# Linear-attention numerators of a perceiver block: one full 128x128 stationary tile per 128 tokens in place of two half tiles

## The reference

```python
qp = exp(q @ W_feat - |q|^2 / 2) / sqrt(128)      # 16 heads of 64, 128 features
kp = exp(k @ W_feat - |k|^2 / 2) / sqrt(128)
def step(carry, qkv):                              # over the 32 tokens of a sequence
    S, z = carry
    q_t, k_t, v_t = qkv
    S = S + einsum('bhd,bhe->bhde', k_t, v_t)
    z = z + k_t
    num = einsum('bhd,bhde->bhe', q_t, S)
    den = einsum('bhd,bhd->bh', q_t, z) + 1e-6
    return ((S, z), num / den[..., None])
y = y @ Wo
```

## Time and profile before

| | |
|---|---|
| median of 3 runs | 260.74 us |
| the three runs | 260.09, 260.74, 263.33 us |
| profiled execution: device time | 261.14 us |
| profiled execution: span | 259.3 us |
| PE busy | 244.4 us, 94% |
| PE weight loads busy | 191.7 us, 74% |
| DVE busy | 186.6 us, 72% |
| ACT busy | 146.4 us, 56% |
| POOL busy | 101.5 us, 39% |

### The profile page before, as it was taken

One profiled execution on the slowest core, in us unless ns is written; L12 is line 12 of the kernel. 1 busy time (PEld: TensorE's weight loads), 2 busy tenths in 40 slices (PEclk: granted clock), 3 DMA queues, 4 the chain that ended last, 5 costly groups with the idle time before them and its releaser, 6 DMA issues.

```text
span 259.3 us, 7034 instructions
## 1 busy us (share of the span) xinstructions
PE 244.4 (94%) x2746; PEld 191.7 (74%) x2752; DVE 186.6 (72%) x474; ACT 146.4 (56%) x284; POOL 101.5 (39%) x139
## 2 busy tenths in 40 slices
PE   7979999999999999999999999999969889999984
PEld 7844467786687678777777778787758778888853
DVE  3586688676833686777887897856556879998995
ACT  1333454454445887665776667666707157877772
POOL 2161113342302568335662688365500023434430
PEclk9979799999999999999999999999979999999999
DMA  6999999970079001100110000000000000010001
GB/s 210 374 382 402 396 399 370 379 278 3 1 223 335 10 0 47 40 3 4 40 43 3 4 3 0 3 3 4 3 0 3 3 1 3 0 43 20 21 25 61
DMA packets 15378, 26.83 MB, mean 103 GB/s; under 512 B 1233, under 2 KB 8689, under 8 KB 15345
## 3 DMA queue, kind: packets, MB, share of 16 engines
q1 hardware_dynamic: 14848, 26.28, 28.3%
q10 hardware_dynamic: 496, 0.10, 0.2%
HBM read 25.33 MB, written 1.05 MB: 102 GB/s over the span
## 4 chain that ended last, share of the span: by engine, by line
PE 66%; DVE 17%; issue 5%; POOL 5%; ACT 3%; DMA 2%; SPq 0%; DVEq 0%; POOLq 0%; ACTq 0%
PE b L1331 11%; PE b L1092 7%; PE b L1373 7%; PE b L1093 6%; PE b L1094 6%; PE b L1350 5%; PE b L1254 3%; PE b L1206 3%; PE b L1250 3%; PE b L1257 3%; PE b L1172 2%; DVE yT_lo L964 2%; PE b L1503 2%; DMA xwq<-in_xWq 2%; DVE smk L910 2%
## 5 line engine op out<-in xcount | busy, mean ns | idle before, releaser
L593 ACT ACTIVATE phi<-b 128x512 f32<-128x512 f32 x48 | 26.0, 598 | 15.3 <-PE b L1331 15.3
L842 DVE TENSOR_TENSOR x_lo<-b,x_hi 128x512 fp32r<-128x512 f32 x32 | 21.7, 688 | 16.8 <-ACT x_hi L460 16.7
L343 POOL TENSOR_TENSOR lnr<-lnv,mh 128x1 f32<-128x1 f32 x16 | 8.8, 552 | 60.8 <-DVE lnv L709 60.8
L400 POOL TENSOR_TENSOR sq_lo<-sq_sum,sq_hi 128x512 fp32r<-128x512 f32 x16 | 20.6, 1287 | 25.9 <-ACT sq_hi L460 25.9
L518 ACT ACTIVATE sq<-b 128x512 f32<-128x512 f32 x32 | 19.3, 603 | 18.2 <-PE b L1094 18.2
L394 POOL TENSOR_TENSOR sq_sum<-sq,sq 128x512 f32<-128x512 f32 x16 | 20.7, 1293 | 21.7 <-ACT sq L518 21.7
L1092 PE MATMUL b<-nT_lo,wp_hi 128*128 128x512 f32 x64 | 26.8, 419 | 0.1
L1373 PEld LDWEIGHTS b<-va,smk 128*64 128x64 f32 x512 | 18.3, 142 | 11.3 <-issue 7.2
L1373 PE MATMUL b<-va,smk 128*64 128x65 f32 x512 | 21.8, 232 | 5.0 <-DVE y L932 2.8
L1093 PE MATMUL b<-nT_hi,wp_lo 128*128 128x512 f32 x64 | 25.1, 391 | 0.0
L1094 PE MATMUL b<-nT_hi,wp_hi 128*128 128x512 f32 x64 | 25.0, 391 | 0.0
(11 more groups left out here) (178 smaller groups left out, 628.6 us busy)
## 6 DMA issues: line engine op xcount, KB each, us to landing
cT<-in_ctxT SPq DMA_DIRECT2D x8, 1028.0 KB, 12.0
cn<-in_ctx SPq DMA_DIRECT2D x8, 1024.0 KB, 10.6
wv_raw<-in_aWv SPq DMA_DIRECT2D x1, 1024.0 KB, 14.2
wp_raw<-in_aWq SPq DMA_DIRECT2D x4, 256.0 KB, 4.8
wp_raw<-in_aWk SPq DMA_DIRECT2D x4, 256.0 KB, 5.0
w_raw<-in_w2T SPq DMA_DIRECT2D x1, 1024.0 KB, 5.7
wo<-in_aWo SPq DMA_DIRECT2D x1, 1024.0 KB, 8.3
w_raw<-in_w1T SPq DMA_DIRECT2D x1, 1024.0 KB, 5.1
```

What stands on the lines that cost most here:

```text
L400: nc.gpsimd.tensor_tensor(sq_lo[n % 2][:], sq_sum[:], sq_hi[n % 2][:].bitcast(F32), ALU.subtract).then_inc(sq_l, 1)
L593: nc.scalar.activation(phi(n, a)[:], feature_bank(a), ACT.Exp).then_inc(f_exp, 1)
L842: nc.vector.tensor_tensor(x_lo[n % 2][r][:], proj_bank(n, r), x_hi[n % 2][r][:].bitcast(F32), ALU.subtract).then_inc(x_l, 1)
```

## The change

`numerators(v)` takes the two half tiles of a group as one: the stationary operand is the whole 128 keys by 128 queries of `smk`, with its zeros, and the output is written to all 128 partitions by one matmul. In the code 8 matmuls become 4; the moving operand, 65 columns of `va` on 128 partitions, is what it was, and is read once for a group where it was read twice. Nothing else is edited: the same masks, zeros, waits, banks and order.

```diff
                 for g in range(HALF):
-                    for b in range(P // PT):
-                        mm = pe.matmul(value_bank(v)[PT * b:PT * (b + 1), g * VW:(g + 1) * VW],
-                                       smk[u % 2][:, a * HALF + g, b, :], va[:, HALF * h + g, head, :],
-                                       start=True, stop=True)
+                    mm = pe.matmul(value_bank(v)[:, g * VW:(g + 1) * VW],
+                                   smk[u % 2][:, a * HALF + g].rearrange("p b n -> p (b n)"),
+                                   va[:, HALF * h + g, head, :], start=True, stop=True)
                 mm.then_inc(n_mm, 1)
```

## The result

The changed kernel takes 272.5 us, the median of four runs from 271.18 to 274.18, against 260.41 us before. The ratio is 1.049 with a 95% interval of 1.040 to 1.059. The forecast was 271.0 us, its range 268.0 to 274.5, and the measured time lies in it. Times of a kernel are medians of all its runs; ratios and their intervals leave out the runs more than 1.5% above the kernel's fastest, so a ratio can be smaller than that of two medians. The profiled execution took 271.83 us with a span of 270.0, against 261.14 and 259.3, so 10.7 us are to be found.

What follows compares the result with a forecast made beforehand. PE bounds the slots; behind them the chain alternates between PE and DVE. Terms 7.6 + 0.54 + 0.84 + 0.68 + 0.6 = 10.3 us on the profiled 261.14 give 271.4, 271.0 as median; range 268.0 to 274.5.

Steps and rivals of the forecast that it cites:

- the wide load is the price: Numerators group: eight 128-column loads 0.111 us apart replace eight pairs at 0.058, so each group is 0.42 us longer.
- The tile shape: Equal shapes save 0.15 us a slot ahead of the projections; two new switches around attention cost 0, at most 0.15.
- The sum: Slots 4 to 14: two groups less one saved switch, 0.69 us each, 7.6 us over eleven slots.
- The tail: From slot 15 on: terms of 0.54, 0.84, 0.68, 0 and 0.6 us added to the slots' 7.6.
- The first group of slot 15 with its switch: Slot 15: 0.42 us for the group and 0.12 for the switch to attention, together 0.54.
- Numerators 23: Second group of slot 15: hidden, since PE then idles 2.54 us for DVE's y; adds nothing.
- Numerators 24 to the start of exponents 15: Behind slot 15: numerators 24 and 25 start at 190.52 with exponents following at once, so +0.84 us.
- The clock: Wait behind slot 15: PE stands still 0.3 to 0.4 us less; should the clock hold, 1.65 us return, giving 269.3.
- Half the instructions, half the time: Numerators: instruction count sets the price, so eight instead of sixteen save 0.23 us a group; 253 us, 3 in 100.
- The wide load is as quick as the narrow one: Numerators: 128-column loads cost no more, groups stay the same, only switches are saved; 259.1 us, 6 in 100.
- Loads wait for the running matmul: Numerators: load and matmul run in turn, 0.165 us an instruction, +0.85 a group; 283.4 us, 4 in 100.
- PE is not the bound in the slots: Slots: the 0.69 us vanish in another wait and the time stays within 2%; 1 in 100.

Runs made afterwards that it cites:

- full_wide: The changed kernel with 128 moving columns instead of 65 in each numerators matmul; 272.54 us, ratio 1.043 to the kernel before.
- full_bf16: The changed kernel's full tile with masked scores and values in bf16, one load and one matmul per group of tokens; 248.59 us, ratio 0.954.
- full_fp32r: The full tile with masked scores and values in fp32r and 66 moving columns; 260.48 us, ratio 1.001 to the kernel before.
- the single halves of the change: Two kernels with the full tile for only even v (first_only) or only odd v (second_only); ratios 1.023 and 1.025, slots 7.73 and 7.58 us.
- full_but_23: The changed kernel with numerators 23 alone, the last group of slot 15, left in half tiles; one run, 278.47 us.
- first_only: The kernel before with the full tile only for even v, the numerators ahead of attention; median 268.47 us, ratio 1.023.
- second_only: The kernel before with the full tile only for odd v, the numerators ahead of the projections; 268.66 us, ratio 1.025.

## Why the prediction was right

**The half tiles ran side by side, and the wide load is the price.** Forecast: a group +0.42 us. Measured: 1.11 against 0.69. The distance of the pairs, 0.058 us, is right, though not by the division that gave it: eight pairs have seven distances between them, and 0.47 / 7 is 0.067. The finer view of the kernel before shows the first eight matmuls of a group:

```profile
133.63 0.45 PE L1373 MATMUL b<-va,smk 128*64 128x65 f32 x8
```

The eight behind them add 0.69 - 0.45 = 0.24 us, or 0.06 a pair. The distance behind the first pair is longer by some 0.05 us, and by luck dividing by eight made up for it. In the changed group seven distances of 0.111 against seven of 0.058 are 0.37 us, and the last matmul, about 0.275 us long in place of 0.22, adds the other 0.05.

The mechanism is shown from two sides, by more columns under the same loads (full_wide) and by cheaper loads under the same columns (full_bf16 against full_fp32r).

**The tile shape.** Forecast: 0.15 us saved ahead of the projections, nothing net for the two new changes around `attention`. Measured: the single halves of the change add 0.40 and 0.25 us. The first projection matmul still lasts 0.48, not the 0.39 that I named as its sign. The gap ahead of it did shrink, to 139.52 - (138.61 + 1.10 - 0.28) = 0.09 us from 0.15. These two changes make 0.08 of the 0.15. The rest lies in the last numerator matmul, which is 0.05 us longer now and reaches that much further over the next load. From start to start the whole shows: the second projection matmul starts 1.22 us behind the first start of the numerators (139.83 - 138.61), where it was 0.95 (128.96 - 128.01). That is +0.27, or 0.42 less 0.15.

**The sum.** Forecast: 0.69 us a slot, 7.6 us to slot 15. Measured: 0.65 and 7.15. Of a slot's 0.65, the way from the first numerators to the second has 0.42 and that to the second projection matmul 0.27; the projections behind it take 2.58 us where they took 2.62, and for these 0.04 I have no cause. The tail was forecast at 2.7 us and took 3.2, with errors both ways. The first group of slot 15 with its switch was forecast at 0.54 and took 0.56. Numerators 23 were called hidden behind DVE, +0, and cost 0.56, shown by full_but_23: the list of waits of `masked` holds `n_mm` for the buffer's reuse, and I had counted DVE's work without it. Numerators 24 to the start of exponents 15 were to add 0.84 and added 0.51 (2.44 us to the last end in place of 1.93): the kernel before was at the lower clock for that stretch and the changed kernel only for part of it, as its 0.74 from 199 to 202 us shows. Numerators 26 and 27 were forecast at 0.68 and took 0.64, 28 and 29 at 0 and took -0.06, 30, 31 and what follows at 0.6 and took 0.65. The remaining 0.3 us lie in exponents 15, in whose stretch the clock was low in both kernels but longer in the changed one. All in all the change took 7.15 + 3.2 = 10.35 us in the profile, and 10.3 were forecast. That they agree so closely is luck: the slots came out 0.45 us lower and the tail 0.5 higher. The forecast held by its mechanism and its range, and the median of 272.5 lies 1.5 above it.

**The clock.** I had expected PE's wait behind slot 15 to be shorter and so gave the clock a chance to hold. The wait is 2.52 us, as long as before, since DVE starts its second masking later, and the clock falls. The low end of the range rested on this and wasn't needed. That PE would stand there for 0.3 to 0.4 us less was wrong, for the same reason as numerators 23.

**The rivals.** "Half the instructions, half the time" is out: eight instructions take 1.11 us where sixteen took 0.69, and in bf16 four take 0.29 where eight take 0.32. "The wide load is as quick as the narrow one" is out for float32: 194 ns against 142, and 0.111 us apart. "Loads wait for the running matmul" is out by full_wide. "PE is not the bound in the slots" is out by 85.00 busy of 85.00 us. The Trainium skill, "TensorE: Matmul & The Clock Gate", states in its section "LDWEIGHTS (loading the stationary operand)" that a load takes, in ns, about its number of columns divided by 1.2. For 128 columns that is an estimate of 0.107 us, and the trace agrees with 0.111; so do the fp32r loads at 0.11. For bf16 the measured 0.024 us does not agree, and the same page's section "Weight-path perf modes — Fast Weight Load (FWL) and DoubleRow" gives a faster load for 128 columns of a type that is not float32. For fp32r, which that condition doesn't name, no run here shows one. The half tiles of 64 columns in bf16, at most 0.03 us apart, aren't covered by that condition, and here the measurement decides.

## What to carry to other kernels

Before merging small matmuls into wide ones, look in the trace whether the small ones run in pairs: matmuls on different columns of the array that start a few ns apart already share the time, and merging them takes nothing away. In float32 here the price of a matmul was the longer of its load (0.111 us for 128 stationary columns) and its stream (0.83 ns a moving column), so 64 by 65 twice beside each other is balanced and 128 by 65 is not; where the load binds, the type of the operands decides, and bf16 changed the order of the versions here. A group behind an engine that looks busy is hidden only if no buffer of that engine's next step waits for it.

## What the runs showed that I had not expected

The clock, once it has fallen behind a wait of 2.5 us, stayed at its lower level for quite different lengths: about 3.4 us in the kernel before, 6.8 us in first_only (196.9 to 203.7, at 0.50, PE busy all the while), as long in second_only (PE busy for 5.98 of the 7.00 us shown), 13.7 us in full_but_23, with PE busy all the while again. That last run was 6 us longer than the changed kernel's median. What decides the length wasn't settled.

Nor is it settled when the clock falls. In ten of the eleven profiles without a fill it fell within 1.5 us of the end of that wait. A fill of 2 us of matmuls in the wait kept it at 1.00 in both profiles that had one. But full_bf16 has the same wait, 2.75 us long, and no fill, and its clock stayed at 1.00 too:

```profile
182.47 0.40 PE L1372 MATMUL b<-va,smk 128*128 128x65 bf16 x8 [2.75 <-DVE y L932]
```
```profile
182.50:186.00 3.50, 2.79 (x48) 2.08 (x48) 2.16 (x10) 1.00 (x3) 0.00 (x0) 1.00 0.02 5
```

So the standing PE makes the fall likely, not certain, and two profiles with a fill are few to show that the fill prevents it.

bf16 loads of 64 columns on half tiles go in pairs at most 0.03 us apart, where float32 loads of the same width need 0.056. Whether fp32r half tiles would behave as float32's wasn't tried.
